# Windowed attention behind a MoE on one core: scores of four steps at once, in four row groups and four banks

## The chip, the core and the metric

The program runs on one core of a Trainium2 chip. The metric is the device time of one execution in microseconds (us). A core has five engines: TensorE (PE; its weight loads are listed apart as PEld), VectorE (DVE), ScalarE (ACT), GpSimd (POOL), and SyncE (SP), which here issues most DMAs. Matmuls write to PSUM, eight banks of 128 partitions x 512 fp32. The engines run their own instruction streams and wait for each other by semaphores.

## The reference

With x of 4 x 1024 x 256, xn = layernorm(x), the result is x + attention(xn) + moe(xn). The MoE part isn't touched. The attention:

```python
qkv = (x @ w_qkv).reshape(B, L, 3, 16, 16)          # 16 heads of 16
# blocks of 64 queries; keys and values: the block before and the block itself
scores = jnp.einsum('bhnqd,bhnkd->bhnqk', qb, k_kv) * scale
scores = jnp.where(band_mask, scores, NEG_INF)      # a window of 64
attn = jax.nn.softmax(scores, axis=-1)
ob = jnp.einsum('bhnqk,bhnkd->bhnqd', attn, v_kv)
return ob.transpose(...).reshape(B, L, D) @ w_out
```

## The kernel before

The program has four phases: the layernorm, the routing, eight experts, and from about 455 us on the attention, the only phase that the change touches.

**Units, steps, groups.** The attention walks over 8 units of 512 tokens (half a batch row). A unit has 16 steps. A step takes one pair of heads and four blocks of 64 queries (BLK): for each block a 128x128 tile of scores, two heads x 64 queries by 128 keys. Four steps are a group (GRP): the four head pairs that lie in the four 32-row groups of a q tile. There are 128 steps and 32 groups. Every engine runs a loop over t, the step, and does each stage of the work with a lag of its own.

**The stages of a step.** PE makes the scores (`scores`, L1190, into `psS`). DVE adds the mask, scales, and takes the row maxima (L1115, four a step), from PSUM to `pr`. ACT takes exp in place with the sums (L1082). PE transposes the four tiles into a bank (L1227, `psP`), DVE copies them to `pT` (L1135). For a group: DVE takes reciprocals of the sums (L1123), PE turns them into rows (L1218), DVE copies the rows to `rrow` (L1129), SP sends them to DRAM and broadcasts them back into `rall` (`spread`, L942). PE multiplies the transposed probabilities by v (L1244, `psO`), DVE scales the product with `rall` into `of` (L1145), and ACT and POOL split it into a high and a low fp32r part (L1074, L1041).

**Scores.** `scores(t)` makes two steps, called at every even t for the steps t+2 and t+3, in two row groups with three banks. It waits for the maxima of step t only, so one bank is being filled while DVE reads another. The transposes have two banks in turn.

**Projections.** Beside a unit's steps PE makes the next unit's q, k and v and the output of the unit before: a list of items, spread over the 16 steps by `SHARE`. In step 0 x is transposed, steps 2 to 7 hold q and k (24 matmuls of 512 columns), steps 8 to 11 the output items o, 12 to 15 the v items (24 matmuls of 256 columns each). Two banks `psA` hold them. ACT and DVE read them out: x is split into a high part (ACT) and a residue (DVE, L1099), q is written by ACT in two halves with the heads' parity as scale (L1063), k is copied by DVE (L1103), v by ACT (L1067), and o is added to `res` by DVE (L1092). POOL gathers the experts' rows and adds them to `res`.

**SP's order.** SP runs one list and blocks at each wait. In a unit: the halo of k, a load of normalised rows (`xnr`, 512 KB), the spreads of four groups, between them the store of a finished unit and a load of `res` (512 KB each), and three shifted copies of v.

**On PE** a step is: the transpose of a group's reciprocals, T of an earlier step, V at a group's end, the step's projections, and the scores.

Of the kernel before, what the change touches and what calls it, by code (L numbers as in the profile page):

```python
# [10 lines left out]
fp32 = mybir.dt.float32  # L11
# [807 lines left out]
def attention_phase(nc, m, x, xn_dram, y_dram, out):  # L819
# [16 lines left out]
    O_FIRST = 2 + 2 * KD  # L836
# [28 lines left out]
    with ctx:  # L865
# [5 lines left out]
        xTh, xTl = sb("a_xTh", [P, KD, UL], fp32r), sb("a_xTl", [P, KD, UL], fp32r)  # L871
        qz = [m.q0, sb("a_q1", [P, 2, UB, 2, WIN], fp32)]
# [8 lines left out]
        rsum = sb("a_rsum", [P, PR, BLK], fp32)  # L881
        rrow = [sb(f"a_rrow{i}", [GRP * BLK, P], fp32) for i in range(2)]
# [21 lines left out]
        row_done, row_out = sem("a_row"), sem("a_row_out")  # L904
        rr_in, rall_in = two("a_rr_in"), two("a_rall_in")
        t_done, pT_done = two("a_t_done"), two("a_pT_done")
# [18 lines left out]
        def ended(t):  # L925
            g = lagged(t, LAG_I)
            return [] if g is None else \
                [(g // STEPS, i) + ITEMS[i] for i in done_at[g % STEPS] if present(g // STEPS, i)]
# [6 lines left out]
        def _(sp):  # L935
# [6 lines left out]
            def spread(n):  # L942

                r = n % 2
                sp.wait_ge(row_out, n + 1)
                if n >= 2:
                    sp.wait_ge(rall_in[r], 16 * (n // 2))
                rr = rr_dram[r].rearrange("(c s) (j t) -> s c j t", s=2, j=BLK)
                for s in range(2):
                    sp.dma_start(rr[s], rrow[r][:, s * WIN:(s + 1) * WIN]).then_inc(rr_in[r], 16)  # L950
                sp.wait_ge(rr_in[r], 32 * (n // 2 + 1))
# [14 lines left out]
            def store(w):  # L966
                freed(w + 1, (O_FIRST + UT - 2, O_FIRST + UT - 1))
                sp.dma_start(ov[:, w * UT:(w + 1) * UT, :], res[w % 2][:, :, :]).then_inc(res_out[w % 2], 16)

            for w in range(UNITS):  # L970
                u, first, last = w % 2, w == 0, w == UNITS - 1
                if not last:
                    if not first:
                        sp.wait_ge(s_done, w * STEPS)
                    sp.dma_start(kT[1 - u][:, :, 0:WIN], kT[u][:, :, UL:UL + WIN]).then_inc(halo_in, 16)
                if w < UNITS - 2:
                    sp.wait_ge(item_done[1], count[w, 1] + 1)
                    sp.dma_start(xnr[:, :, :], xnv[:, (w + 2) * UT:(w + 3) * UT, :]).then_inc(xn_in, 16)
                if not first:
                    spread(4 * w - 1)  # L980
                spread(4 * w)
                spread(4 * w + 1)
                if not first:
                    store(w - 1)
                spread(4 * w + 2)
                if not first and not last:
                    sp.wait_ge(res_out[1 - u], 16 * ((w + 1) // 2))
                    sp.dma_start(res[1 - u][:, :, :], xv[:, (w + 1) * UT:(w + 2) * UT, :]).then_inc(res_in[1 - u], 16)
                if not last:
                    freed(w, (NI - 2, NI - 1))  # L990
                    if first:
                        sp.wait_ge(pads, 1)
                    shifts(1 - u)
            spread(GROUPS - 1)
# [5 lines left out]
        def _(pool):  # L1000
# [10 lines left out]
            for t in range(ALL + LAG_L + 1):  # L1011
# [26 lines left out]
                n = group_at(t, LAG_L)  # L1038
                if n is not None:
                    pool.wait_ge(o_high, n + 1)  # L1040
# [4 lines left out]
        def _(act):  # L1045
# [4 lines left out]
            def read_item(w, i, kind, j):  # L1050
# [10 lines left out]
                elif kind == "q":  # L1061
                    for s in range(2):
                        ins = act.activation(qz[u][:, j, :, s, :], psA[bank][:, :].rearrange("p (n t) -> p n t", n=UB),  # L1063
                                             ACT.Copy, scale=parity[:, s:s + 1])
                    ins.then_inc(item_free[bank], 1)
# [4 lines left out]
            for t in range(ALL + LAG_H + 1):  # L1070
                n = group_at(t, LAG_H)
                if n is not None:
                    act.wait_ge(o_full, n + 1)
                    act.activation(o_cols(oTh, n), of[:, n % 2, :], ACT.Copy).then_inc(o_high, 1)  # L1074
# [11 lines left out]
        def _(dve):  # L1086
# [20 lines left out]
            for t in range(ALL + LAG_M + 1):  # L1107
                if t < ALL:
                    r = t % PR
                    if t >= PR:  # L1110
                        dve.wait_ge(t_done[t % 2], (t - PR) // 2 + 1)
                    alone(dve, s_done, t + 1)
                    for j in range(BLK):
                        band = 1 if t % (2 * STEPS) < STEPS and t // GRP % 2 == 0 and j == 0 else 0
                        dve.tensor_tensor_reduce(  # L1115
                            out=pr[:, r, j, :], in0=psS[bank_of[t % 4]][:, j * P:(j + 1) * P],
                            in1=m.mask[:, band, :], scale=-(DH ** -0.5), scalar=BIG,
                            op0=ALU.add, op1=ALU.min, accum_out=nmax[:, r, j:j + 1]).then_inc(max_done, 1)
                n = group_at(t, LAG_RS)
                if n is not None:  # L1120
                    slots = slice(n % 2 * GRP, (n % 2 + 1) * GRP)
                    dve.wait_ge(exp_done, (n + 1) * GRP * BLK)
                    dve.reciprocal(rsum[:, slots, :], sums[:, slots, :]).then_inc(rsum_done, 1)  # L1123
                n = group_at(t, LAG_SC)
                if n is not None:
                    dve.wait_ge(row_done, n + 1)
                    if n >= 2:
                        dve.wait_ge(rr_in[n % 2], 32 * (n // 2))
                    dve.tensor_copy(rrow[n % 2][:, :], psR[0:GRP * BLK, 0:P]).then_inc(row_out, 1)  # L1129
                g = lagged(t, LAG_C)  # L1130
                if g is not None:
                    dve.wait_ge(t_done[g % 2], g // 2 + 1)
                    if g >= PTR:
                        dve.wait_ge(pv_done, (g - PTR) // GRP + 1)
                    dve.tensor_copy(pT[:, g % PTR, :, :].rearrange("p c q -> p (c q)"), psP[g % 2][:, :])\  # L1135
                        .then_inc(pT_done[g % 2], 1)
                for w, i, kind, j in ended(t):
                    read_item(w, i, kind, j)
                n = group_at(t, LAG_M)
                if n is not None:  # L1140
                    dve.wait_ge(pv_done, n + 1)
                    dve.wait_ge(rall_in[n % 2], 16 * (n // 2 + 1))
                    if n >= 2:
                        dve.wait_ge(o_low, n - 1)
                    dve.tensor_tensor(of[:, n % 2, :], psO[:, 0:BLK * WIN], rall[n % 2][:, :], ALU.mult)\  # L1145
                        .then_inc(o_full, 1)
            for i in range(O_FIRST, O_FIRST + UT):
                add_out(UNITS, i, ITEMS[i][1])

        @block.tensor  # L1150
        def _(pe):
# [38 lines left out]
            def scores(t):  # L1190
                w, u, s = t // STEPS, t // STEPS % 2, t % STEPS
                if s == 0:
                    for i in (O_FIRST - 2, O_FIRST - 1):
                        pe.wait_ge(item_free[i % 2], i // 2 + 1 if w == 0 else count[w - 1, i] + 1)
# [4 lines left out]
                mt, half = s // (2 * GRP), s // GRP % 2  # L1199
# [12 lines left out]
            for t in range(ALL + LAG_V + 1):  # L1212
                n = group_at(t, LAG_SC)
                if n is not None:

                    pe.wait_ge(rsum_done, n + 1)
                    pe.wait_ge(max_done, min(t, ALL) * BLK)
                    pe.transpose(psR[0:GRP * BLK, 0:P],  # L1218
                                 rsum[:, n % 2 * GRP:(n % 2 + 1) * GRP, :].rearrange("p c j -> p (c j)"), m.eye[:, :])\
                        .then_inc(row_done, 1)  # L1220
                g = lagged(t, LAG_T)
                if g is not None:
                    pe.wait_ge(exp_done, (g + 1) * BLK)
                    if g >= 2:
                        pe.wait_ge(pT_done[g % 2], g // 2)
                    for j in range(BLK):
                        ins = pe.transpose(psP[g % 2][:, j * P:(j + 1) * P], pr[:, g % PR, j, :], m.eye[:, :])  # L1227
                    ins.then_inc(t_done[g % 2], 1)
                n = group_at(t, LAG_V)
                if n is not None:  # L1230
# [4 lines left out]
                    for i in (0, 1):  # L1235
                        pe.wait_ge(pT_done[i], (n + 1) * GRP // 2)
# [12 lines left out]
                if t < ALL:  # L1249
                    for i in range(NI):  # L1250
                        parts = [part for item, part in parts_at[t % STEPS] if item == i]
                        if parts and present(t // STEPS, i):
                            product(t // STEPS, i, parts)
                if t % 2 == 0 and t + 2 < ALL:
                    n = group_at(t, LAG_SC)
                    if n is not None:
                        pe.wait_ge(row_out, n + 1)
                    scores(t + 2)
# [68 lines left out]
```

## Time and profile before

| | |
|---|---|
| median of 3 runs | 750.66 us (749.59 to 751.91) |
| profiled execution | 753.59 us, its span from first to last instruction 751.8 |
| mean granted TensorE clock | 0.958 of full speed |
| busy, share of the span | PE 93%, ACT 62%, DVE 60%, POOL 46% |
| attention, from the first scores to the end | 455.3 to 751.8 us |

A row of a timeline or of the chain gives start and length in us, the engine, the line, what is written from what, and how many instructions were put together (x16). Busy times of matmuls include their modelled ends, so they overlap; the chain cuts them so that its pieces add up.

### The profile page before, as it was taken

The page shows a single profiled execution, that of the slowest core. Times are in us where ns is not written, and L with a number is a line of the kernel's source. Part 1 is how long each engine was busy: PE and PEld are TensorE (multiplying, and loading weights), DVE is VectorE, ACT ScalarE, POOL GpSimd, SP SyncE. Part 2 cuts the span into 40 slices and gives each one's busy share as a digit, 9 for nine tenths or more (in the row PEclk, how much of TensorE's full clock was granted, in tenths as well). Part 3 has the DMA queues.
Part 4 walks back from the last instruction along what each step waited for, and adds up shares of the span by engine and source line. Part 5 has one row for each costly group of instructions (what it writes and reads, how often), then busy time and mean ns, then how long its engine had stood idle before and what let it go on. Part 6 is the DMA issues. An engine that isn't in the chain of part 4 may idle for free. (4 is left out here: it accounts for less than half of the span.)

```text
span 751.8 us, 20032 instructions
## 1 busy us (share of the span) xinstructions
PE 695.6 (93%) x6872; PEld 605.8 (81%) x6873; DVE 449.2 (60%) x1678; ACT 469.3 (62%) x1503; POOL 348.2 (46%) x482
## 2 busy tenths in 40 slices
PE   6563999999999999999999998999999999999784
PEld 3352799898998989989899896888898888888673
DVE  7982442534425344253442514888888988888872
ACT  4652652916529165291652905998989889898960
POOL 4646451524525245252452306366655656555740
PEclk8986899999999999999999997999999999999977
DMA  9735042222422224222241014142534526252411
GB/s 307 263 104 166 11 127 80 78 94 70 130 80 79 88 70 133 83 77 84 70 133 36 0 44 144 39 119 81 153 114 113 145 76 181 74 132 73 126 64 36
DMA packets 57946, 76.60 MB, mean 102 GB/s; under 512 B 8208, under 2 KB 50448, under 8 KB 57872
## 3 DMA queue, kind: packets, MB, share of 16 engines
q1 hardware_dynamic: 51376, 58.83, 25.3%
q0 software_dynamic: 6144, 16.79, 7.6%
q8 instruction: 41, 0.67, 0.4%
q14 instruction: 33, 0.27, 0.1%
q10 hardware_dynamic: 352, 0.04, 0.0%
HBM read 51.95 MB, written 17.04 MB: 92 GB/s over the span
## 5 line engine op out<-in xcount | busy, mean ns | idle before, releaser
L1082 ACT ACTIVATE a_p<-a_p,a_nmax 128x128 f32<-128x128 f32 x512 | 198.3, 396 | 31.0 <-DVE a_nmax L1115 30.2
L750 DVE TENSOR_TENSOR m_hl<-m_hf,m_hh 128x512 fp32r<-128x512 f32 x128 | 93.3, 729 | 99.6 <-ACT m_hh L707 99.6
L66 PE MATMUL m_psY<-m_w2h,m_hh 128*128 128x256 f32 x512 | 145.0, 283 | 0.0
L66 PE MATMUL m_psY<-m_w2l,m_hh 128*128 128x256 f32 x512 | 143.9, 281 | 0.0
L66 PE MATMUL m_psY<-m_w2h,m_hl 128*128 128x256 f32 x512 | 143.8, 281 | 0.0
L703 ACT ACTIVATE m_hf<-m_psF,b1T 128x512 f32<-128x512 f32 x128 | 88.2, 689 | 65.9 <-PE m_psF L66 50.8
L1115 DVE CUSTOM_DVE_ANT_0 a_p<-a_psS,mask 128x128 f32<-128x128 f32 x512 | 116.4, 278 | 20.9 <-PE a_psS L1205 15.1
L671 POOL CAST m_w2h<-raw 128x256 fp32r<-128x256 f32 x64 | 25.9, 405 | 177.6 <-PE m_psY L66 120.6
L66 PE MATMUL m_psF<-m_xh,w1h 128*128 128x512 f32 x256 | 103.5, 404 | 1.9 <-DVE m_xl L727 1.9
L66 PE MATMUL m_psF<-m_xl,w1h 128*128 128x512 f32 x256 | 101.8, 398 | 0.0
L66 PE MATMUL m_psF<-m_xh,w1l 128*128 128x512 f32 x256 | 101.8, 398 | 0.0
L1082 ACT ACTIVATION_READ_ACCUMULATOR a_p<-a_p,a_nmax 128x1 f32 x512 | 100.0, 195 | 0.0
L66 PEld LDWEIGHTS m_psY<-m_w2h,m_hh 128*128 128x128 f32 x512 | 96.5, 188 | 0.4
L66 PEld LDWEIGHTS m_psY<-m_w2l,m_hh 128*128 128x128 f32 x512 | 96.5, 188 | 0.3
L66 PEld LDWEIGHTS m_psY<-m_w2h,m_hl 128*128 128x128 f32 x512 | 96.5, 189 | 0.0
L736 DVE TENSOR_TENSOR y<-m_psY,b2b 128x256 f32<-128x256 f32 x64 | 27.2, 425 | 113.2 <-PE m_psY L66 113.2
L691 ACT ACTIVATE m_xh<-m_psT 128x512 fp32r<-128x512 f32 x32 | 19.1, 599 | 111.7 <-PE m_psT L772 99.0
L1227 PE MATMUL a_psP<-eye,a_p 128*128 128x128 f32 x512 | 81.8, 284 | 6.4 <-DVE a_pT L1135 6.4
L707 ACT ACTIVATE m_hh<-m_psF,b1T 128x512 fp32r<-128x512 f32 x128 | 87.2, 681 | 0.0
L1135 DVE COPY a_pT<-a_psP 128x512 f32<-128x512 f32 x128 | 84.5, 661 | 0.9 <-PE a_psP L1227 0.9
L1227 PEld LDWEIGHTS a_psP<-eye,a_p 128*128 128x128 f32 x512 | 58.4, 144 | 19.2 <-ACT a_p L1082 7.7
L1041 POOL TENSOR_TENSOR a_oTl<-a_o,a_oTh 128x256 fp32r<-128x256 f32 x32 | 23.4, 731 | 107.9 <-ACT a_oTh L1074 107.9
(192 smaller groups left out, 1403.2 us busy)
## 6 DMA issues: line engine op xcount, KB each, us to landing
raw<-in_L_ffn_w SPq DMA_DIRECT2D x16, 1024.0 KB, 5.5
y_scratch<-y SPq DMA_DIRECT2D x64, 128.0 KB, 1.7
n_xin<-in_L_attn_x SPq DMA_DIRECT2D x8, 512.0 KB, 7.8
xn_scratch<-n_xn SPq DMA_DIRECT2D x8, 512.0 KB, 7.6
a_res<-in_L_attn_x SPq DMA_DIRECT2D x8, 512.0 KB, 4.7
a_rall<-recip_scratch SPq DMA_DIRECT2D x32, 128.0 KB
out<-a_res SPq DMA_DIRECT2D x8, 512.0 KB, 3.3
xnr<-xn_scratch SPq DMA_DIRECT2D x7, 512.0 KB, 6.3
```

The costliest lines, as they stand in the source:

```text
L66: last = pe.matmul(out, a, b, start=(n_start and i == 0), stop=(n_stop and i == n - 1))
L671: pool.tensor_copy(w2h[:, c, :], raw2[:, c, :]).then_inc(w2h_done, 1)
L691: act.activation(xh[:, g % KD, (g // KD) * HALF:(g // KD + 1) * HALF], psT[g % 2][:, :], ACT.Copy)\
L703: act.activation(hf[:, u % FR, :], psF[u % 4][:, :], ACT.Relu, bias=bias)
L707: act.activation(hh[:, u // HC, u % HC, :], psF[u % 4][:, :], ACT.Relu, bias=bias)\
L736: dve.tensor_tensor(yb[:, s % YR:s % YR + 1, :], psY[s % 2][:, 0:D].unsqueeze(1), m.b2b[:, bass.ds(e, 1), :], ALU.add).then_inc(yb_done, 1)
L750: dve.tensor_tensor(hl[:, u // HC, u % HC, :], hf[:, u % FR, :], hh[:, u // HC, u % HC, :].bitcast(fp32), ALU.subtract).then_inc(hl_done, 1)
L1041: pool.tensor_tensor(o_cols(oTl, n), of[:, n % 2, :], o_cols(oTh, n).bitcast(fp32), ALU.subtract)\
L1082: act.activation(e, e, ACT.Exp, scale=-1.0, bias=nmax[:, r, j:j + 1], accum_out=sums[:, r, j:j + 1]).then_inc(exp_done, 1)
L1115: dve.tensor_tensor_reduce(out=pr[:, r, j, :], in0=psS[bank_of[t % 4]][:, j * P:(j + 1) * P], in1=m.mask[:, band, :], scale=-(DH ** -0.5), ...
L1135: dve.tensor_copy(pT[:, g % PTR, :, :].rearrange("p c q -> p (c q)"), psP[g % 2][:, :])\
L1227: ins = pe.transpose(psP[g % 2][:, j * P:(j + 1) * P], pr[:, g % PR, j, :], m.eye[:, :])
```

## The change

- One call of `scores` makes a whole group: four steps in four row groups, each with a bank of its own. It is called at the end of every fourth step and waits until all maxima of the group before are done.
- The scores had three banks and T two; now the scores have four and T has one, so T of a step waits for the copy of the step before.
- The reciprocals aren't turned by PE and copied by DVE: DVE transposes them in blocks of 32x32 into a `rrow` of 128x32. They go to DRAM in four transfers, not two.
- q: ACT copies once into `qp`, POOL writes the two halves. The rounding of the attention's product to its high part moves from ACT to POOL.
- The o items come after the v items. The lags change: T's copy and V come one step earlier, M and the split one later. V stands behind the scores in PE's step.
- SP's list: the store is one unit later and stands ahead of the load of normalised rows; the load of `res` follows the unit's first spread.

```diff
-    LAG_I, LAG_RS, LAG_T, LAG_C, LAG_SC, LAG_V, LAG_M, LAG_H = 1, 2, 3, 4, 3, 5, 7, 8
-    LAG_YS, LAG_YA, LAG_L = 5, 6, 9
+    LAG_I, LAG_Q, LAG_RS, LAG_T, LAG_C, LAG_V, LAG_M, LAG_H = 1, 2, 2, 3, 3, 4, 8, 9
+    LAG_YS, LAG_YA, LAST = 5, 6, 10
     ITEMS = [("x", 0), ("x", 1), ("q", 0), ("k", 0), ("q", 1), ("k", 1)] + \
-        [("o", t) for t in range(UT)] + [("v", t) for t in range(UT)]
+        [("v", t) for t in range(UT)] + [("o", t) for t in range(UT)]
...
-        psS = [ps(f"a_psS{i}") for i in range(3)]
-        bank_of = (0, 1, 0, 2)
-        psR = psS[1]
-        psP = [ps("a_psP0"), ps("a_psP1")]
+        psS = [ps(f"a_psS{i}") for i in range(GRP)]
+        psP = ps("a_psP")
...
-                for s in range(2):
-                    sp.dma_start(rr[s], rrow[r][:, s * WIN:(s + 1) * WIN]).then_inc(rr_in[r], 16)
+                for q in range(4):
+                    rows = slice(32 * q + GRP * BLK * r, 32 * q + GRP * BLK * (r + 1))
+                    sp.dma_start(to[:, :, q // 2, q % 2, :], rrow[r][rows, :]).then_inc(rr_in[r], 16)
...
                 if not last:
                     if not first:
-                        sp.wait_ge(s_done, w * STEPS)
+                        sp.wait_ge(s_done, w * STEPS + GRP)
                     sp.dma_start(kT[1 - u][:, :, 0:WIN], kT[u][:, :, UL:UL + WIN]).then_inc(halo_in, 16)
+                if w > 1:
+                    store(w - 2)
                 if w < UNITS - 2:
                     sp.wait_ge(item_done[1], count[w, 1] + 1)
                     sp.dma_start(xnr[:, :, :], xnv[:, (w + 2) * UT:(w + 3) * UT, :]).then_inc(xn_in, 16)
                 if not first:
                     spread(4 * w - 1)
+                if w > 1:
+                    sp.wait_ge(res_out[u], 16 * (w // 2))
+                    sp.dma_start(res[u][:, :, :], xv[:, w * UT:(w + 1) * UT, :]).then_inc(res_in[u], 16)
                 spread(4 * w)
                 spread(4 * w + 1)
-                if not first:
-                    store(w - 1)
-                spread(4 * w + 2)
-                if not first and not last:
-                    sp.wait_ge(res_out[1 - u], 16 * ((w + 1) // 2))
-                    sp.dma_start(res[1 - u][:, :, :], xv[:, (w + 1) * UT:(w + 2) * UT, :]).then_inc(res_in[1 - u], 16)
                 if not last:
-                    freed(w, (NI - 2, NI - 1))
+                    freed(w, (O_FIRST - 2, O_FIRST - 1))
...
                     shifts(1 - u)
+                spread(4 * w + 2)
+            store(UNITS - 2)
             spread(GROUPS - 1)
             store(UNITS - 1)
...
+                for w, i, kind, j in ended(t, LAG_Q):
+                    if kind == "q":
+                        pool.wait_ge(item_free[i % 2], count[w, i] + 1)
+                        for s in range(2):
+                            ins = pool.tensor_scalar(qz[(w + 1) % 2][:, j, :, s, :],
+                                                     qp[:, j, :].rearrange("p (n t) -> p n t", n=UB),
+                                                     parity[:, s:s + 1], 0.0, ALU.mult, ALU.add)
+                        ins.then_inc(q_done, 1)
+                n = group_at(t, LAG_H)
                 if n is not None:
+                    pool.wait_ge(o_full, n + 1)
+                    pool.tensor_copy(o_cols(oTh, n), of[:, n % 2, :]).then_inc(o_high, 1)
                     pool.wait_ge(o_high, n + 1)
...
+                n = group_at(t, LAG_RS)
+                if n is not None:
+                    half = n % 2
...
+                    dve.wait_ge(exp_done, (n + 1) * GRP * BLK)
+                    dve.reciprocal(rsum[:, half * GRP * BLK:(half + 1) * GRP * BLK].rearrange("p (c j) -> p c j", j=BLK),
+                                   sums[:, half * GRP:(half + 1) * GRP, :]).then_inc(rsum_done, 1)
+                    dve.wait_ge(rsum_done, n + 2)
+                    if n >= 2:
+                        dve.wait_ge(rr_in[half], 64 * (n // 2))
+                    dve.transpose(rrow[half][:, :], rsum[:, :]).then_inc(row_out, 1)
+                g = lagged(t, LAG_C)
+                if g is not None:
+                    dve.wait_ge(t_done, g + 1)
+                    if g >= PTR:
+                        dve.wait_ge(pv_done, (g - PTR) // GRP + 1)
+                    dve.tensor_copy(pT[:, g % PTR, :, :].rearrange("p c q -> p (c q)"), psP[:, :])\
+                        .then_inc(pT_done, 1)
...
-            def scores(t):
-                w, u, s = t // STEPS, t // STEPS % 2, t % STEPS
+            def scores(n):
+
+                w, u, i = n * GRP // STEPS, n * GRP // STEPS % 2, n % (STEPS // GRP)
...
-                if t > 0:
-                    pe.wait_ge(max_done, (t - 1) * BLK)
+                if n > 0:
+                    pe.wait_ge(max_done, n * GRP * BLK)
...
-                    for i in range(2):
-                        c = (s + i) % GRP
+                    for c in range(GRP):
                         rows = slice(32 * c, 32 * c + 32)
-                        ins = pe.matmul(psS[bank_of[(t + i) % 4]][:, j * P:(j + 1) * P],
+                        ins = pe.matmul(psS[c][:, j * P:(j + 1) * P],
...
                 g = lagged(t, LAG_T)
                 if g is not None:
                     pe.wait_ge(exp_done, (g + 1) * BLK)
-                    if g >= 2:
-                        pe.wait_ge(pT_done[g % 2], g // 2)
+                    if g > 0:
+                        pe.wait_ge(pT_done, g)
                     for j in range(BLK):
-                        ins = pe.transpose(psP[g % 2][:, j * P:(j + 1) * P], pr[:, g % PR, j, :], m.eye[:, :])
-                    ins.then_inc(t_done[g % 2], 1)
+                        ins = pe.transpose(psP[:, j * P:(j + 1) * P], pr[:, g % PR, j, :], m.eye[:, :])
+                    ins.then_inc(t_done, 1)
+                if t < ALL:
+                    for i in range(NI):
...
+                            product(t // STEPS, i, parts)
+                if t % GRP == GRP - 1 and t + 1 < ALL:
+                    scores((t + 1) // GRP)
                 n = group_at(t, LAG_V)
```

DVE's step after the change is, in this order: the maxima of t, M, the reciprocals and their transpose, the copy of step t - 3, the read-outs of items. PE's: T of step t - 3, the projections, the scores, V.

## Rows read from the trace of the kernel before

**Rows 1.** Busy us of PE, PEld, DVE, ACT, POOL in units 1, 7; clock, DMA share.
```profile
491.99:526.37 34.38, 34.38 (x533) 29.51 (x534) 30.15 (x165) 30.99 (x144) 20.52 (x29) 1.00 0.36 106
...
698.27:729.40 31.13, 25.76 (x392) 21.94 (x392) 24.52 (x143) 24.60 (x123) 17.19 (x25) 0.89 0.37 103
```

**Rows 2.** The chain that ended last, unit 5: start, us, what.
```profile
630.53 1.09 PE a_psS L1205 x16
631.62 0.59 PE a_psP L1227 x4
...
632.32 0.44 PE a_psP L1227 x4
632.76 0.93 PE a_psA L1183 x4
...
636.73 1.03 PE a_psO L1244 x64
...
649.65 0.71 PE a_psA L1183 x6
```

**Rows 3.** Timeline of DVE where it waits for nothing, unit 7.
```profile
701.18 0.40 DVE L1145 TENSOR_TENSOR a_o<-a_psO,a_rall 128x256 f32<-128x256 f32 x1
701.51 0.27 DVE L1115 CUSTOM_DVE_ANT_0 a_p<-a_psS,mask 128x128 f32<-128x128 f32 x1
...
702.35 0.67 DVE L1135 COPY a_pT<-a_psP 128x512 f32<-128x512 f32 x1
702.95 0.27 DVE L1115 CUSTOM_DVE_ANT_0 a_p<-a_psS,mask 128x128 f32<-128x128 f32 x1
...
705.23 0.23 DVE L1123 RECIPROCAL a_rsum<-a_sums 128x16 f32<-128x16 f32 x1
705.40 0.61 DVE L1135 COPY a_pT<-a_psP 128x512 f32<-128x512 f32 x1
```

**Rows 4.** The chain, three stretches: handovers, and scores at a low clock.
```profile
455.29 1.18 PE a_psS L1205 x16
...
456.61 0.29 DVE a_p L1115
...
711.14 0.61 DVE a_pT L1135
...
715.39 2.01 PE a_psS L1205 x16
...
730.16 1.07 PE a_psP L1227 x4
```

**Rows 5.** Timelines of PE and DVE; in brackets the idle time ahead.
```profile
711.89 0.63 PE L1227 MATMUL a_psP<-eye,a_p 128*128 128x128 f32 x4 [2.83 <-DVE a_pT L1135]
...
731.26 0.69 DVE L1135 COPY a_pT<-a_psP 128x512 f32<-128x512 f32 x1 [0.41 <-PE a_psP L1227]
...
739.66 0.42 DVE L1145 TENSOR_TENSOR a_o<-a_psO,a_rall 128x256 f32<-128x256 f32 x1 [3.77 <-issue]
```

**Rows 6.** Groups of instructions, the attention: count, busy us, mean ns.
```profile
L1026 POOL TENSOR_SCALAR a_yg<-a_yg,gates 128x256 f32<-128x256 f32 x64 | 30.7, 480 | 0.9 <-DMA a_yg<-y_scratch,slots 0.9
...
L1092 DVE TENSOR_TENSOR a_res<-a_res,a_psA 128x256 f32<-128x256 f32 x32 | 13.0, 406 | 7.0 <-PE a_psA L1183 6.9
...
L1099 DVE TENSOR_TENSOR a_xTl<-a_psA,a_xTh 128x512 fp32r<-128x512 f32 x14 | 9.0, 686 | 4.4 <-ACT a_xTh L1060 4.4
```

**Rows 7.** Timeline of SP's DMA issues: a spread behind a load, the last spread.
```profile
530.82 1.36 SPq L950 DMA_DIRECT2D recip_scratch<-a_rrow  x2
536.46 0.62 SPq L954 DMA_DIRECT2D a_rall<-recip_scratch  x1
...
734.39 1.29 SPq L950 DMA_DIRECT2D recip_scratch<-a_rrow  x2
736.80 0.62 SPq L954 DMA_DIRECT2D a_rall<-recip_scratch  x1
```

**Rows 8.** Busy time by stretch, after the longest gap in unit 7.
```profile
712.00:719.00 7.00, 7.00 (x98) 6.21 (x98) 4.08 (x26) 4.47 (x24) 3.94 (x6) 0.58 0.17 49
```

More of the change, by code:

```diff
@@ L871, in attention_phase @@
         xTh, xTl = sb("a_xTh", [P, KD, UL], fp32r), sb("a_xTl", [P, KD, UL], fp32r)
+        qp = sb("a_qp", [P, KD, UL], fp32)
         qz = [m.q0, sb("a_q1", [P, 2, UB, 2, WIN], fp32)]
@@ L880, in attention_phase @@
         sums = sb("a_sums", [P, PR, BLK], fp32)
-        rsum = sb("a_rsum", [P, PR, BLK], fp32)
-        rrow = [sb(f"a_rrow{i}", [GRP * BLK, P], fp32) for i in range(2)]
+        rsum = sb("a_rsum", [P, 2 * GRP * BLK], fp32)
+        rrow = [sb(f"a_rrow{i}", [P, 2 * GRP * BLK], fp32) for i in range(2)]
         rall = [sb(f"a_rall{i}", [P, BLK * WIN], fp32) for i in range(2)]
@@ L903, in attention_phase @@
         max_done, exp_done, rsum_done = (sem(f"a_{n}") for n in ("max", "exp", "rsum"))
-        row_done, row_out = sem("a_row"), sem("a_row_out")
+        row_out = sem("a_row_out")
         rr_in, rall_in = two("a_rr_in"), two("a_rall_in")
-        t_done, pT_done = two("a_t_done"), two("a_pT_done")
+        t_done, pT_done = sem("a_t_done"), sem("a_pT_done")
+        q_done = sem("a_q_done")
         pv_done = sem("a_pv_done")
@@ L923, in group_at, with ended @@
             return g // GRP if g is not None and g % GRP == GRP - 1 else None
-        def ended(t):
-            g = lagged(t, LAG_I)
+        def ended(t, lag=LAG_I):
+            g = lagged(t, lag)
             return [] if g is None else \
@@ L1009, in row_of @@
                 return g // 2, g // STEPS, i // K, i % K
-            for t in range(ALL + LAG_L + 1):
+            for t in range(ALL + LAST):
                 g = lagged(t, 0)
@@ L1061, in read_item @@
                 elif kind == "q":
[L1062 to L1065, printed above, removed]
+                    if w > 0:
+                        act.wait_ge(q_done, KD * (w - 1) + j + 1)
+                    act.activation(qp[:, j, :], psA[bank][:, :], ACT.Copy).then_inc(item_free[bank], 1)
                 else:
@@ L1068, in read_item @@
                                    ACT.Copy).then_inc(item_free[bank], 1)
[L1070 to L1074, printed above, removed]
+            for t in range(ALL + LAST):
                 for w, i, kind, j in ended(t):
@@ L1105, in read_item @@
                     add_out(w, i, j)
-            for t in range(ALL + LAG_M + 1):
+            dve.memset(rsum[:, :], 1.0).then_inc(rsum_done, 1)
+            for t in range(ALL + LAST):
                 if t < ALL:
@@ L1110, in _ @@
                     if t >= PR:
-                        dve.wait_ge(t_done[t % 2], (t - PR) // 2 + 1)
+                        dve.wait_ge(t_done, t - PR + 1)
                     alone(dve, s_done, t + 1)
@@ L1115, in _ @@
                         dve.tensor_tensor_reduce(
-                            out=pr[:, r, j, :], in0=psS[bank_of[t % 4]][:, j * P:(j + 1) * P],
+                            out=pr[:, r, j, :], in0=psS[t % GRP][:, j * P:(j + 1) * P],
                             in1=m.mask[:, band, :], scale=-(DH ** -0.5), scalar=BIG,
                             op0=ALU.add, op1=ALU.min, accum_out=nmax[:, r, j:j + 1]).then_inc(max_done, 1)
[L1119 to L1138, printed above, removed]
                 n = group_at(t, LAG_M)
@@ L1146, in _ @@
                         .then_inc(o_full, 1)
+                n = group_at(t, LAG_RS)
+                if n is not None:
+                    half = n % 2
+                    if n == 0:
+                        dve.wait_ge(rsum_done, 1)
+                    dve.wait_ge(exp_done, (n + 1) * GRP * BLK)
[12 more added lines that the diff above has]
+                        .then_inc(pT_done, 1)
+                for w, i, kind, j in ended(t):
+                    read_item(w, i, kind, j)
             for i in range(O_FIRST, O_FIRST + UT):
@@ L1188, in _ @@
                 pe.sem_inc(item_done[i], PRO // 2)
-            def scores(t):
-                w, u, s = t // STEPS, t // STEPS % 2, t % STEPS
-                if s == 0:
-                    for i in (O_FIRST - 2, O_FIRST - 1):
-                        pe.wait_ge(item_free[i % 2], i // 2 + 1 if w == 0 else count[w - 1, i] + 1)
+            def scores(n):
+                w, u, i = n * GRP // STEPS, n * GRP // STEPS % 2, n % (STEPS // GRP)
+                if i == 0:
+                    if w > 0:
+                        pe.wait_ge(q_done, KD * w)
+                    for k in ((V_FIRST - 2, V_FIRST - 1) if w == 0 else (V_FIRST - 3, V_FIRST - 1)):
+                        pe.wait_ge(item_free[k % 2], k // 2 + 1 if w == 0 else count[w - 1, k] + 1)
                     if w > 0:
                         pe.wait_ge(halo_in, 16 * w)
-                if t > 0:
-                    pe.wait_ge(max_done, (t - 1) * BLK)
-                mt, half = s // (2 * GRP), s // GRP % 2
+                if n > 0:
+                    pe.wait_ge(max_done, n * GRP * BLK)
+                mt, half = i // 2, i % 2
                 for j in range(BLK):
                     blk = half * BLK + j
-                    for i in range(2):
-                        c = (s + i) % GRP
+                    for c in range(GRP):
                         rows = slice(32 * c, 32 * c + 32)
-                        ins = pe.matmul(psS[bank_of[(t + i) % 4]][:, j * P:(j + 1) * P],
+                        ins = pe.matmul(psS[c][:, j * P:(j + 1) * P],
                                         qz[u][rows, mt, blk, :, :].rearrange("p s t -> p (s t)"),
@@ L1211, in _ @@
             scores(0)
[L1212 to L1220, printed above, removed]
+            for t in range(ALL + LAST):
                 g = lagged(t, LAG_T)
@@ L1223, in _ @@
                     pe.wait_ge(exp_done, (g + 1) * BLK)
-                    if g >= 2:
-                        pe.wait_ge(pT_done[g % 2], g // 2)
+                    if g > 0:
+                        pe.wait_ge(pT_done, g)
                     for j in range(BLK):
-                        ins = pe.transpose(psP[g % 2][:, j * P:(j + 1) * P], pr[:, g % PR, j, :], m.eye[:, :])
-                    ins.then_inc(t_done[g % 2], 1)
+                        ins = pe.transpose(psP[:, j * P:(j + 1) * P], pr[:, g % PR, j, :], m.eye[:, :])
+                    ins.then_inc(t_done, 1)
+                if t < ALL:
+                    for i in range(NI):
+                        parts = [part for item, part in parts_at[t % STEPS] if item == i]
+                        if parts and present(t // STEPS, i):
+                            product(t // STEPS, i, parts)
+                if t % GRP == GRP - 1 and t + 1 < ALL:
+                    scores((t + 1) // GRP)
                 n = group_at(t, LAG_V)
@@ L1234, in _ @@
                         pe.wait_ge(shift_in, 48 * (w + 1))
-                    for i in (0, 1):
-                        pe.wait_ge(pT_done[i], (n + 1) * GRP // 2)
+                    pe.wait_ge(pT_done, (n + 1) * GRP)
                     if n > 0:
@@ L1248, in _ @@
                     ins.then_inc(pv_done, 1)
[L1249 to L1258, printed above, removed]
             for i in range(O_FIRST, O_FIRST + UT):
```

10 lines of the change are left out of this document (5 added, 5 removed).

## The prediction, on record before the run

> **What bounds the kernel now.** I looked first at the stretches of the attention stage, one for each of its eight units of 16 steps [rows 1]. Unit 1 is shown; units 2 to 6 repeat it to the hundredth: 34.38 us each, TensorE busy for all of it at full clock, DVE for 30.15, ACT for 30.99, POOL for 20.52. So TensorE sets the pace of units 0 to 6, and two other engines stand within 12% of it. The last unit has no projections left and isn't bound by TensorE. Then I read the chain of work inside one unit [rows 2]. It never leaves TensorE, so its pieces are prices: a scores call S (two steps, two row groups) 1.09, the four transposes T of a step 0.44 after a projection and 0.59 after S, a projection share p 0.93 in steps 2 to 7 and 0.71 in steps 8 to 15, the value products V of a group 1.03. The 16 instructions of S take 0.068 each where a transpose with as many columns takes 0.11: two row groups already overlap. V's 64 instructions take 0.016 each, in four column groups. Third, DVE where nothing holds it up [rows 3], read from start to start: the four maxima of a step 0.84, the copy of T's result 0.60 (its record ends after 0.67), the reciprocal 0.17 (record 0.23), the scaling M 0.33. Last, the handovers [rows 4, 5]: copy end to T 0.14 and a T that starts idle 0.63; S end to the first maximum 0.14; T end to the copy 0.03.
>
> **What the change does to the engines.** S for four steps is 32 instructions in eight waves of four instead of 16 in eight waves of two. If four row groups overlap as two do, it stays at 1.09, and a unit has four of them, not eight: TensorE loses 4 x 1.09 = 4.4 us a unit, besides the transposes of the sums and a few changes from S to T at 0.15. That alone would take the bound from 34.4 to about 29. ACT loses work (o's rounding, one of two q copies), POOL gets it: four 128x512 scalings at twice the 0.48 of a 128x256 one [rows 6] and four small copies at no more than that, 5.8 us on 20.5, under 27 of any unit. Both stay off the path. DVE exchanges the copy of a row for its own transpose, and loses the wait for TensorE between them.
>
> **What it does to the order.** The price is in the buffers. Two score banks ahead of DVE become none: S(n) fills all four banks, so it waits until all maxima of the group before are done, and the maxima wait until S ends, since every bank gets its last block at the end. The transposes have one bank instead of two: T of a step waits for DVE's copy of the step before. So the engines wait for each other in a loop. Call the step that ends with S s0 (t mod 4 = 3), the next ones s1, s2, s3. From the end of the copy in s3, on TensorE: 0.14 to wake up, T 0.63, p, S 1.09, V 1.03 (V now stands between S and the next T), T of s1 0.59, 0.03 to the copy: 3.51 + p. In s0 DVE has M and a copy for that time and then waits for S; in s1 it takes its maxima 1.32 after S begins, done at 2.16, and waits again, as T of s1 comes only behind V, at 2.74. Then DVE sets the pace: copy 0.60, maxima of s2 0.84, reciprocal and transpose 0.50, copy 0.60, maxima of s3 0.84, copy 0.67 to its end: 4.05. TensorE has its T and p of s2 and s3 ready by then. The loop is 7.56 + p + what DVE has to read out in s1 to s3.
>
> A unit has four loops. p in the four s0 is 0.93 twice and 0.71 twice: 3.28. The read-outs: two x residues and two k copies of 128x512 like the copy, at 0.60, and three of the four additions for o, which are as long as M (0.406 against 0.40), at 0.33 [rows 6, 3]; the fourth falls into s0 and is hidden. That is 3.39. The unit: 4 x 7.56 + 3.28 + 3.39 = 36.9, against 34.38: **2.5 us more**, and 17.6 over units 0 to 6. The S that TensorE saves isn't lost; it is spent waiting.
>
> The reciprocal's 0.50 is 0.23 to its end, an estimated 0.07 until the transpose may start, and 0.20 for the transpose of 128x32, an operation that this trace doesn't show. Its bounds are nothing and the 0.60 of a 512-column copy; I take 0.20 as the nearest row is the reciprocal, 0.17 with half the columns. Over 28 loops the bounds are -6 and +11 us. The Trainium skill, VectorE: DVE Perf Modes, The three transpose paths, gives 311 ns for a DVE transpose of 128x128 bf16; no run here shows one, and by it the sum would be 3 us higher. V after S may cost a change of 0.15 (T does): 0 to +4.
>
> **The last unit and the end.** Without p, S waits for DVE's maxima of s0, some 0.37 later than T would allow: 7.93 a loop. The unit is then three loops and the last maxima, about 31; it was 31.13 with some 5 us of stall in it [rows 1], and I put it at no change. At the end the last reciprocals go out in four transfers instead of two. Two issues took 1.29 [rows 7], so 1.3 more; a store of 512 KB is now queued just ahead of them on SP, which costs 0 to 3 (a spread behind a load went from 2.4 to 5.6 us between its first issue and the next [rows 7]). I take +2 in all.
>
> **SP's order.** In units 2 to 5, ahead of a unit's first spread, stand a store and a load, then another load. Its issue to scaling took 5.6 us behind one load, then 2.9 for the broadcast [rows 7, 5]; with 1.3 for two more issues and 3.2 for the store, as much as that load added, it is 13.0. M now comes six steps after the reciprocals, not four: 13.8 us at 9.2 a loop, less some 2 for which SP still issues the load. DVE idles about 1 us in s0 anyway, which covers a late M. So nothing, with little to spare.
>
> **The sum.** 17.6 + 0 + 2 = 19.6 us. Against the profiled execution (753.59, a span of 751.8 and 1.8 around it) that is 773; its own time stands 2.9 above the median, so on 750.66 I say **770**. With the bounds above the forecast's own range is 764 to 785.
>
> **The rivals.**
> - *Faster: the loop doesn't close.* If DVE gets far enough ahead not to feel S and V, only its own work counts: 16 x 1.44 + 4 x 0.83 + 2.4 + 1.32 = 30.1 a unit, 4.3 less, 723 in all. For it: TensorE's gain is real and DVE has gaps [rows 1]. Against it: one bank set each way leaves no step to get ahead by. It decides where the loop's mean falls below 34.38 / 4 = 8.60; mine is 9.23. Chance 0.10. The Trainium skill, TensorEngine Tiling, PSUM Bottleneck, says that tiling speeds up TensorE but not evacuation, which may become the limit; by that rule alone DVE's 30.1 would be the time of a unit.
> - *Break-even*, 0.63 a loop shorter, 751. Chance 0.04.
> - *A spread comes late* and M holds DVE: 2 us a unit, 784. Chance 0.12.
> - *The clock falls.* After 2.83 us without matmuls [rows 5] TensorE ran for 7 us at a granted 0.58, most of it on the lower of its two levels, 1.2 GHz instead of 2.4 [rows 8], and S took 2.01 [rows 4]. TensorE will idle more, most in the last unit; with S 0.92 longer, and by the same factor two T 0.5 and V 0.87, its four loops cost 11 more, 781. Against it: the gaps are under 1 us. Chance 0.07.
> - *Four row groups don't overlap*, so S is 2.18: 32 x 1.09 = 35 more, 805. Against it: two do, and four column groups in V. Chance 0.05.
>
> **The numbers.** The forecast has 0.62. The range leaves out the two faster or equal cases and the failed overlap (0.19): 757 to 788. A measurement of this kernel tells about 0.3% from no change. Slower by more: 0.62 + 0.12 + 0.07 + 0.05 = 0.86; within it 0.04; faster 0.10.
>
> **What the profile will show.** A unit of about 37 us with TensorE busy some 80 to 85% of it, and no engine full; scores calls of 32 instructions in 1.1 us; twice in four steps a wait of DVE, for S about 1 us and for T about 0.6; T waiting for the copy in s3 and s0. I am wrong if units come out below 34.4, if S takes 2 us, or if DVE's longest waits are for the reciprocals' broadcast.

## The result, and the profile after

The changed kernel takes **776.1 us** (774.97 to 777.04) against 751.3 for the kernel before on the same chip: a ratio of 1.033, 95% interval 1.031 to 1.036. The forecast was 770, slower, in a range of 757 to 788. The profiled execution took 775.4, a span of 773.5.

Two units by stretch, unit 4 (from the start of its first S to that of unit 5) and the last unit, columns as in [rows 1]:

```profile
core 0: us, PE busy (x) PEld busy (x) DVE busy (x) ACT busy (x) POOL busy (x), PEclk, DMA share, GB/s
...
603.11:639.59 36.48, 31.00 (x530) 25.20 (x529) 30.33 (x165) 29.17 (x138) 24.81 (x36) 1.00 0.39 113
...
714.88:749.00 34.12, 24.33 (x453) 19.69 (x452) 25.05 (x142) 23.61 (x117) 21.06 (x31) 0.80 0.24 76
```

A unit is 36.48 instead of 34.38 [rows 1], and now no engine fills it: TensorE has lost 3.4 us of work and is busy 85%, DVE 83%. The profile's chain of work through one group, from the T of s0 to the next one (S takes its place between s0 and s1):

```profile
611.62 0.63 PE a_psP L1231 x4
612.25 0.94 PE a_psA L1193 x4
613.19 1.10 PE a_psS L1217 x32
614.29 1.03 PE a_psO L1254 x64
615.32 0.60 PE a_psP L1231 x4
615.92 0.02 issue
615.94 0.06 DVE a_pT L1153
...
617.48 0.17 DVE a_rsum L1142
...
617.81 0.06 DVE a_pT L1153
...
618.97 0.28 DVE a_p L1124
...
619.29 0.66 ACT a_p L1090 x3
...
619.99 0.58 ACT a_p L1090 x3
620.57 0.07 issue
620.64 0.63 PE a_psP L1231 x4
```

In [rows 2] the chain never left TensorE; here it goes T, p, S, V, T on TensorE, then over to DVE for s1 to s3, and back. The way back leads over ACT in this view, and that piece misleads, as shown below: what T of s0 waits for is DVE's copy. S for four steps is 32 instructions in 1.10, where 16 took 1.09. What DVE waits for in units 2 to 5, as sum, number and longest:

```profile
DVE a_p L1124 <- issue: 14.9, 16, 1.3
DVE a_pT L1153 <- PE a_psP L1231: 9.6, 16, 0.7
```

Once in each of 16 groups the first maximum waits (for S, which this view calls issue: 614.44 below lies 0.15 behind the end of S's 1.17), 0.93 on average, and once the copy waits for T, 0.60. The view lists no other wait of DVE; the reciprocals' broadcast doesn't appear. One group on DVE's row, with its wait for S and the copy's wait for T:

```profile
614.44 0.29 DVE L1124 CUSTOM_DVE_ANT_0 a_p<-a_psS,mask 128x128 f32<-128x128 f32 x1 [1.20 <-issue]
...
615.94 0.69 DVE L1153 COPY a_pT<-a_psP 128x512 f32<-128x512 f32 x1 [0.57 <-PE a_psP L1231]
...
617.39 0.25 DVE L1142 RECIPROCAL a_rsum<-a_sums 128x16 f32<-128x16 f32 x1
617.67 0.21 DVE L1147 STREAM_TRANSPOSE a_rrow<-a_rsum 128x32 f32<-128x32 f32 x1
...
619.81 0.68 DVE L1153 COPY a_pT<-a_psP 128x512 f32<-128x512 f32 x1
```

The same group on TensorE's row, where T of the next s0 comes behind the copy of s3, and the end of the exponentials that this T reads, on ACT's row:

```profile
613.12 1.17 PE L1217 MATMUL a_psS<-k,q 32*128 32x128 f32 x32
...
620.64 0.63 PE L1231 MATMUL a_psP<-eye,a_p 128*128 128x128 f32 x4 [0.48 <-ACT a_p L1090]
...
622.14 1.17 PE L1217 MATMUL a_psS<-k,q 32*128 32x128 f32 x32
```

```profile
616.24 0.19 ACT L1090 ACTIVATION_READ_ACCUMULATOR a_p<-a_p,a_nmax 128x1 f32 x1
```

The copy of s3 ends at 619.81 + 0.68 = 620.49 and T starts 0.15 later, the handover of [rows 4]. The column and the chain name ACT instead, but the exponentials that end just before this T belong to a later step. Its own are those of the maxima at 614.44, three steps earlier, and they ended at 616.43, 4.2 before it. In units 2 to 5 this distance is never under 4.0, so no T waits for its exponentials; experiment 10 tests the same.

Where the time went, from S to S in the two profiled executions: unit 0 +1.9 (32.8 to 34.7), units 1 to 6 +17.0 (206.3 to 223.3), the last unit and the end +1.2 (57.5 to 58.7). The rest of the span's 21.7 is 1.6 ahead of attention, where nothing was changed: over all traces of this case, the first S starts anywhere between 455.2 and 457.3.

### The profile page after: what moved, and what is told of

It reads as the page before. It is cut to its first block and busy times, and to the rows that moved or that the text cites. A ratio compares the mean times of both kernels' runs of the same rounds, so it can differ in the third digit from the quotient of the medians.

```text
span 773.5 us, 19999 instructions
## 1 busy us (share of the span) xinstructions
PE 672.0 (87%) x6840; PEld 576.2 (74%) x6841; DVE 451.2 (58%) x1679; ACT 455.7 (59%) x1457; POOL 380.3 (49%) x542
## 5 line engine op out<-in xcount | busy, mean ns | idle before, releaser
L1231 PE MATMUL a_psP<-eye,a_p 128*128 128x128 f32 x512 | 83.8, 288 | 44.7 <-ACT a_p L1090 26.8
L1231 PEld LDWEIGHTS a_psP<-eye,a_p 128*128 128x128 f32 x512 | 56.1, 144 | 70.6 <-ACT a_p L1090 61.0
L1153 DVE COPY a_pT<-a_psP 128x512 f32<-128x512 f32 x128 | 87.0, 679 | 26.3 <-PE a_psP L1231 25.9
L1090 ACT ACTIVATION_READ_ACCUMULATOR a_p<-a_p,a_nmax 128x1 f32 x512 | 95.9, 187 | 0.0
L1021 POOL DMA_INDIRECT a_yg<-y_scratch,slots x64 | 64.3, 1005 | 11.6 <-issue 9.3
```

What stands on the lines that cost most here:

```text
L1021: pool.indirect_dma_start(yg[n % YG][:, :], None, y_dram, bass.IndirectOffsetOnAxis(ap=m.slots[:, c:c + 1], axis=0))\
L1090: act.activation(e, e, ACT.Exp, scale=-1.0, bias=nmax[:, r, j:j + 1], accum_out=sums[:, r, j:j + 1]).then_inc(exp_done, 1)
L1231: ins = pe.transpose(psP[:, j * P:(j + 1) * P], pr[:, g % PR, j, :], m.eye[:, :])
```

## The experiments

All are edits of the changed kernel or of the kernel before; the ratios are to the kernel before. The cuts of code are shortened to what changes, and their comments, which give the order of work in a step, are added here.

**1. V later.** The value products go behind the next step's T:

```diff
-LAG_V = 4    # T, p, S, V
+LAG_V = 5    # T, V, p, S
```

> The value products V move one step later, behind the next step's transposes T, and nothing else. Theory (closed loop between DVE and TensorE): T of s1 no longer stands behind V's 1.03, ends 1.68 after S begins instead of 2.74, and DVE goes from its maxima (done at 2.16) straight to the copy, so each loop loses 0.6 us: 28 loops by 0.6 are 17, 776 becomes about 759, a unit 34. Rival (DVE's amount of work sets the time): 776. Rival (T waits for ACT's exponentials, as the column of releasers says): 776.

**752.0** (1.001, 0.999 to 1.002): 24 less, all that the change had cost, with both changes of banks still in place. Units 1 to 6 take 209.5 instead of 223.3 (34.8 in unit 4), near the 0.6 a loop expected. DVE's waits for T in units 2 to 5 fall from 9.6 to 2.1. Another 8.2 come from the last unit, which ran at full clock, granted 1.00, where the changed kernel had 0.80 [rows 8 show the kernel before there]:

```profile
699.80:733.92 34.12, 24.99 (x549) 20.11 (x548) 30.87 (x168) 26.54 (x133) 24.39 (x37) 1.00 0.29 90
```

So V between S and T was paid in full, and DVE's sum of work isn't the limit. The total equals that of the kernel before by two differences that cancel: units 1 to 6 are still 3.2 longer (209.5 against 206.3), and the last unit with the end is 7.0 shorter (50.5 against 57.5).

**2. S first.** In s0, S goes ahead of p.

> In the step s0 the scores S go ahead of that step's projection share p, nothing else. Theory (closed loop): S starts some 0.7 earlier, but p now stands between S and T of s1, so the copy of s1 comes 0.9 later after S; the two cancel and the time stays within 3 us of 776. Rival (only the way from the maxima to S counts, the transposes are hidden): 0.7 less in 28 loops, 756.

**785.9** (1.046): 10 more, 38.4 to 38.8 a unit. Neither came out, but the sign speaks for the loop: S came earlier, DVE's waits for it in units 2 to 5 fell from 14.9 to 6.1, and its waits for T rose from 9.6 to 26.4, because p and V now both stand ahead of T of s1. I had cancelled the two and overrated what S gains: it still waited 0.54 for s0's maxima.

**3. Both,** V and the p of s0 behind T of s1.

> S goes ahead of p in s0, V and that p go behind T of s1; T, S, T, V, p, p is then the order of TensorE around S. Theory: the loop loses both p and V. From the start of the copy in s3: maxima 0.60 to 1.44 while T runs, S 1.58 to 2.67, maxima of s1 2.81 to 3.65, then DVE without a gap to the next copy of s3 at 6.95; with 0.85 of read-outs 7.8 a loop, 31.2 a unit instead of 36.5: 5.3 by 7 units is 37 less, about 738, and DVE is over 90% busy. Rival (DVE's amount of work): 776. Rival (clock): PE has more gaps and the granted clock falls, above 750.

**766.6** (1.021), 36.3 in units 3 and 4, not 31.2. DVE's line in s2 shows one reason:

```profile
612.00 0.69 DVE L1153 COPY a_pT<-a_psP 128x512 f32<-128x512 f32 x1 [1.21 <-PE a_psP L1231]
```

V and two shares of p in a row make the next T late; in units 2 to 5 DVE waits 8.0 for T. It also waits 9.7 for products that it has to read out (o and k), as these shares of p come later. My theory had watched only the way through S; with one bank of transposes every step is such a way.

**4. Two row groups at a time,** in the same four banks, called as far ahead as in the kernel before:

```diff
-    for c in range(GRP):
+    for c in (t % GRP, t % GRP + 1):
...
-if t % GRP == GRP - 1 and t + 1 < ALL: scores((t + 1) // GRP)
+if t % 2 == 0 and t + 2 < ALL: scores(t + 2)
```

> One part undone: the four score banks are filled by two row groups at a time, two steps a call, a call every second step, as far ahead as in the kernel before; the one bank of transposes, DVE's transposes of the reciprocals and POOL's splits stay. Theory (the loop closes because all four score banks are filled at once): DVE is a bank pair behind again, TensorE is the bound, a unit takes 34.4 less the sums' transposes (about 0.5 to 1.0), 33.5 to 34.4, 755 to 761 in all. Rival (the one bank of transposes closes the loop by itself): 776. Rival (the work moved to POOL and DVE costs it): 776.

**773.9** (1.031), 37.45 a unit. The theory as I had put it here falls: with the score banks open again 2 us are won, not 15 to 21. DVE waits for S no more in units 2 to 5, and for T 39 times, 26.9 in all. This edit also gives back what four row groups had saved TensorE, which is busy 35.0 a unit instead of 31.0; the unit stands 3.1 above that of the kernel before all the same. With V between S and T as here, the single bank of transposes closes the loop by itself.

**5. One bank of transposes in the kernel before.**

```diff
-psP = [ps("a_psP0"), ps("a_psP1")]
+psP = [ps("a_psP0")] * 2
```

> The kernel before with one bank of transposes instead of two, T of a step waiting for the copy of the step before, nothing else changed. Theory (the bank of transposes by itself closes a loop): the engines meet in every step, and a unit takes 37 (as with two row groups and one bank) to 41, since S here comes behind the same wait: 770 to 800. Rival (only the scores filled four at once close the loop): TensorE stays the bound, 751 to 755.

**829.1** (818.7 to 833.1; 1.096), 44 to 45 a unit: more than the range. Every second T now stands still for a copy (0.55 here, 1.06 for the next; this copy had ended at 619.61, so the name ACT is wrong again). S is queued behind T, V and p, and DVE, which has to finish maxima that need this S before its next copy, waits in turn:

```profile
619.76 0.63 PE L1227 MATMUL a_psP<-eye,a_p 128*128 128x128 f32 x4 [0.55 <-ACT a_p L1082]
...
622.25 1.16 PE L1205 MATMUL a_psS<-a_k,a_q 32*128 32x128 f32 x16
```

```profile
623.58 0.29 DVE L1115 CUSTOM_DVE_ANT_0 a_p<-a_psS,mask 128x128 f32<-128x128 f32 x1 [2.09 <-issue]
```

The changed kernel gets away with 36.48 in one bank, I think because its copy follows T in the same step and S comes once in four; no run shows this by itself. Nor could the counterpart be run as it stands, the changed kernel with two banks of transposes: four banks for scores, two for projections, one each for transposes and value products fill all eight.

**6 and 7. The other parts alone,** in the kernel before: DVE's transposes with four transfers; POOL's splits of q and o.

> The kernel before with one part of the change: reciprocals turned by DVE in the step of the reciprocals and sent out in four transfers; no transposes of sums on TensorE, no wait of S for that row. Theory: TensorE bounds these units, so it gains what four small transposes and the changes around them cost it, 0.1 to 0.3 each: 0.4 to 1.2 a unit, 743 to 748. Rival (DVE's transposes or the two more transfers are what costs): 755 or more.

> The kernel before with the other part: q copied once by ACT and split by POOL, o rounded by POOL. Theory: off the path, 751 within 2. Rival (POOL's work costs it: later q or later o for the projections): 755 or more.

**746.6** (0.993, 0.990 to 0.996) and **752.4** (1.002, 1.000 to 1.004). The first is a small gain, in the range but not by the way expected: in the profiled execution 0.2 in a full unit (less than the 0.4 expected at least) and 4.9 from the last unit's first S on, whose cause stays open. The second is nothing. So neither part explains the 25 us. SP's new order, the o items behind the v items and the lags other than V's weren't undone one by one; experiment 1 keeps them all and is back at the time before.

**8, 9 and 10. The same work in three places** of the changed kernel: a copy of a score bank to an unused tile on DVE, in s1 or in s2, each time just ahead of the copy of T's result (in s2 behind the reciprocals, not ahead of them as the expectation says), and four unused copies of 128x128 on ACT.

```diff
+if t < ALL and t % GRP == 0:   # s1; 1 and psS[1] for s2
+    dve.tensor_copy(spare[:, :], psS[0][:, :])
```

> The changed kernel with one copy of a score bank (128x512, 0.60 on DVE) added to every group, in s1 between the maxima and the copy, its result unused. Theory (TensorE and DVE meet in every step, and what counts is the slower of the two in that step): in s1 DVE waits 0.57 to 0.65 for T behind V, so the added 0.60 disappears: 776 to 778. Rival (DVE's amount of work sets the time): 32 by 0.60, 19 more, 795.

> The same copy added in s2, between the maxima and the reciprocals' step of DVE's row, where T is ready and TensorE waits for DVE. Theory: it is paid in full, 0.60 in each of 32 loops, 17 to 20 more: 793 to 796. Rival (DVE has gaps of over 1 us in a group and fits it in): 776 to 780.

> The changed kernel with four unused 128x128 copies on ACT in every group, one ahead of each exponential of s2, some 0.3 each, 1.2 a group. Theory (the exponentials run three steps ahead of T, and the releaser that the views name for T, ACT, is only the last event before the start): nothing, 775 to 778. Rival (T does wait for the exponentials): up to 1.2 in 32 groups, 795 to 815.

**776.0, 796.8 and 776.1** (1.032, 1.062, 1.032). The lines of DVE, in s1 and in s2:

```profile
605.72 0.69 DVE L1150 COPY a_spare<-a_psS 128x512 f32<-128x512 f32 x1
606.33 0.68 DVE L1156 COPY a_pT<-a_psP 128x512 f32<-128x512 f32 x1
```

```profile
605.63 0.65 DVE L1150 COPY a_spare<-a_psS 128x512 f32<-128x512 f32 x1
606.19 0.68 DVE L1156 COPY a_pT<-a_psP 128x512 f32<-128x512 f32 x1
```

In s1 the copy fills the wait for T, which has gone from its line (9.6 in units 2 to 5 became 1.1), and costs nothing. In s2 it costs 20.7 by the medians, a little more than expected; its four runs spread from 792.0 to 801.1, and the profiled one, the 792.0, is 16.6 longer than that of the changed kernel. There unit 3 went from 36.48 to 38.80, 0.58 a group: all of the 0.56 from the copy's start to the next one's. On ACT 1.2 a group cost nothing: T doesn't wait for the exponentials, as the distance of 4.0 and more had said, and the column's name for it was wrong.

**11. Reordered.** S ahead of p in s0, V in s2, DVE's read-outs ahead of its copy:

```diff
-LAG_V = 4    # T, p, S, V;  DVE: maxima, M, copy, read-outs
+LAG_V = 6    # T, S, V, p;  DVE: maxima, M, read-outs, copy
```

> The changed kernel with three moves: S ahead of p in s0, V two steps later (in s2, ahead of that step's p), and DVE's read-outs of projections ahead of its copy. Theory now held (one bank of transposes makes TensorE and DVE meet in every step, and four score banks filled at once make them meet again in s0: a step lasts as long as the slower engine, so the work must lie where the other engine is busy too): in s0 TensorE has only T, S and p, V falls into s2 where DVE has its longest step (copy, maxima, reciprocal, transposes), and about 1 us of each group's 9.1 is won: 32 to 33.5 a unit, 742 to 752 in all. Rival (TensorE's order matters only where it stands between S and T of s1): V's move alone gave 34.8 a unit, S first gave 38.4, so 752 or more.

**744.7** (0.990, 0.987 to 0.993), 33.6 to 34.3 in units 1 to 6. The total lies in the range, the unit above it; the last unit, at full clock again, makes up for it. The same S first that cost 10 in experiment 2 does no harm here, where V no longer stands behind it: the whole is 7 less than with V's move alone. What each of the three moves is worth by itself wasn't run.

**12. Shares.** The same, with the parts of p spread so that steps with V hold fewer:

```diff
-SHARE = [4, 0, 4, 4, 4, 4, 4, 4] + [3] * 8
+SHARE = [4, 2, 4, 3, 4, 3, 4, 4, 4, 1, 3.5, 2.5, 4, 2, 4, 3]
```

> The reordered kernel with the projections' parts spread over the steps by what TensorE has else in each: fewer in the steps that hold V, more in the steps before, the sum the same. Theory: each of these steps ends later by what TensorE exceeds DVE there; 0.5 to 0.9 a unit is won, 739 to 742 against 744.7. Rival (the shares don't matter, TensorE's sum does): 745.

**735.6** (0.979, 0.976 to 0.981): faster than both kernels, 40 us below the changed one with the same instructions in another order, and 3 below the range that I expected. By stretch:

```profile
584.87:617.28 32.41, 30.94 (x529) 25.38 (x529) 30.34 (x165) 28.78 (x138) 24.59 (x37) 1.00 0.49 135
683.04:717.16 34.12, 25.27 (x552) 20.41 (x553) 31.30 (x169) 26.57 (x134) 24.43 (x37) 1.00 0.34 103
```

Above, unit 4 and the first 34 us of the last unit: in 32.41 TensorE does 30.94 and DVE 30.34, the same work as in the 36.48 of the changed kernel, with TensorE now at 95%. DVE's waits in units 2 to 5 are 5.4 for S and 2.2 for T.

## Why the prediction was right

The direction, the unit and the loop came out as worked; the total is close in part by luck, as the last points show.

- **S.** 1.09 forecast, 1.10 measured: the rival of four row groups that don't overlap is out.
- **The loop.** By the working the four groups of a unit last 10.0, 9.1, 8.9 and 8.9; in unit 4 they took 10.01, 9.02, 8.86 and 8.59. The unit is 36.48 instead of 36.9. Most of the difference is one addition for o that was counted and is free: in s3 it stands behind the copy, so T of s0 doesn't wait for it (copy at 637.49, addition at 638.09, T at 638.32). DVE's transpose was put at 0.20; the copy behind it starts 0.14 after it (617.67, 617.81), which makes 0.42 of the 0.50 for reciprocal and transpose. The waits are as foretold: S about 1 us, T about 0.6, once a group each.
- **TensorE's sum** was put at about 29 a unit. It is 31.0; as TensorE isn't the limit here, this had no part in the time.
- **The cause** was put in two places, four score banks filled at once and one bank of transposes. Experiment 4 takes the first away and next to nothing comes back; experiment 5 shows that in the kernel before the second alone costs more than the whole change. Yet neither has to cost anything: with both in place, V's move alone brings the time back (experiment 1), and other orders go below it (11, 12). What the change cost is the loss of the right to work ahead together with the order in which the work stands. V's place, named in the loop at 1.03, was the cheapest way out, and 8 against 9 show the rule behind it.
- **DVE's 30.1 as a bound** (the faster rival) was not reached by the change, since neither engine can work ahead; the 32.41 of experiment 12 comes within 2.3 of it. The Trainium skill, TensorEngine Tiling, PSUM Bottleneck, says that after tiling the copies out of PSUM may become the bottleneck. Here that holds in another form: not DVE's sum sets the time (83% busy), but where its work stands in the loop.
- **POOL and ACT** were put off the path. POOL's scalings took 1.36 a pair and not 1.92, and its time is 24.8 a unit, not 26.3; that cost nothing, as experiment 7 shows for the kernel before.
- **SP's order** cost nothing: DVE has no wait for the broadcast in units 2 to 5. The late spread is out. The working was luckier than it looks: its 13.0 against 13.8 less 2 and plus 1 leaves nothing to spare at all. But from a unit's first issue of a spread to its broadcast it had 10.1, and the trace has 4.7 (608.24 to 612.94; M that needs it runs at 621.25).
- **The clock.** The rival (chance 0.07) put its fall into the last unit, and against it stood that the gaps are under 1 us. That was wrong: TensorE stands for 1.53, 1.19 and 1.19 there, and S takes 2.09, 1.88 and 2.09.

```profile
720.70 0.63 PE L1231 MATMUL a_psP<-eye,a_p 128*128 128x128 f32 x4 [1.53 <-ACT a_p L1090]
...
723.22 2.09 PE L1217 MATMUL a_psS<-a_k,a_q 32*128 32x128 f32 x32
```

  The three loops of that unit took 8.34, 8.69 and 9.95 instead of 7.93 each, 3.2 more. The term still came out at +1.2, with +2 forecast, since the kernel before had a low clock there too (0.89 [rows 1]) and a stop of 2.83 [rows 5]; that the two are nearly equal is luck. The clock also fell at the end of unit 0, which has no output projections to fill TensorE, 0.92 granted in 484 to 491, then 0.53 in 491 to 497:

```profile
490.59 1.08 PE L1231 MATMUL a_psP<-eye,a_p 128*128 128x128 f32 x4 [0.88 <-DVE a_pT L1153]
491.60 2.09 PE L1217 MATMUL a_psS<-a_k,a_q 32*128 32x128 f32 x32
```

  S at 2.09 is S at the lower of the two levels, 1.2 instead of 2.4 GHz. Unit 1 took 38.29, 1.8 above units 3 and 4.
- **The 6 us missing** from the forecast are 2.1 by which the span grew more than forecast (21.7, not 19.6), 3.1 because the profiled execution before stood 2.3 above its median and that after 0.8 below, and 0.6 between the two medians of the kernel before. The 2.1 is what is left of larger errors that cancel. The loops added 14.9 (17.6 forecast). Units 1 and 6 (38.29 and 38.68 instead of 36.48) added another 4.0, 3.3 of it in their first groups, and 1.6 lies ahead of attention; no term held either. The end added 1.2 (2 forecast). In unit 6 TensorE stood for 1.47 between the first and the second of a T's weight loads (678.33, 679.87), when the copy and the exponentials that T waits for had ended 3.0 and 6.8 before. The same stop comes at the same place in experiment 10; why stays open.

## What to carry to other kernels

Two engines that hand one buffer back and forth can't average over steps: each step lasts as long as the slower of the two in it, so before giving a bank away, ask which engine then loses the right to work ahead. Where the bank is gone, order pays: put each engine's long pieces into the steps in which the other is long too (experiments 1, 11 and 12 moved 24, 31 and 40 us with the same instructions; 8 to 9 of each came in the last unit, where the clock rose too). To learn what a wait is worth, put the same spare piece of work into two places: free in one, full price in the other, tells more than any column of releasers.

## What the runs showed of the hardware

- The last unit's clock went with the order of the work: granted 1.00 over its first 34 us in experiments 1, 11 and 12, against 0.80 in the changed kernel, where TensorE stood for over 1 us three times. From its first S to the end it took 50.5, 50.3 and 49.4, against 58.7: the waits seem to be paid twice there, as time and as clock. How much each had of the difference wasn't measured.
- DVE's transpose of 128x32 in 32-bit floats lasts 0.21 in the record, and the next operation starts 0.14 after it. The Trainium skill, VectorE: DVE Perf Modes, The three transpose paths, has 311 ns for 128x128 in bf16, a shape that no run here shows.
